# A four-layer cross-attention and mixture-of-experts kernel: middle attentions re-ordered, layernorms and a close by halves, rows numbered by partition, offsets in one load

## The chip, the cores and the metric

The kernel runs on one core of a Trainium2 chip. The metric is the device time of one launch in microseconds (us): lower is better. TensorE (PE, with its weight loads shown as PEld), VectorE (DVE), ScalarE (ACT), GpSimd (POOL) and SyncE (SP) run their own instruction streams and meet at semaphores. Each instruction waits in its stream for the one before it.

## The reference

A residual stream x of 4 batches x 256 tokens x 128 features goes through four layers. Each is a cross attention over a context of 64 rows per batch and a feed-forward network with experts, each behind a layernorm:

```python
x = x + _L0_xattn_ref(_layernorm(x), ctx, ctx, bias, ...)      # 16 heads of 8, additive bias, softmax
x = x + _L0_ffn_ref(_layernorm(x), Wr, W1, W2)                 # 8 experts, top 2, capacity 320, relu
x = x + _L1_xattn_ref(ctx, ctx, _layernorm(x), fm_w, fm_b, fc_w, fc_b)
    # per head z = fm_w @ h + fm_b, features [exp(z), exp(-z)] of q, k and v; softmax(q k / sqrt(128)) v
x = x + _L1_ffn_ref(_layernorm(x), gate_w, Wg, Wu, Wd, Sg, Su, Sd)
    # each of 16 experts takes its 128 best tokens; gelu(g) * u; plus a shared expert
x = x + _L2_xattn_ref(_layernorm(x), ctx, ctx, mask, ...)      # scores clipped to +-50, exp / sum
x = x + _L2_ffn_ref(_layernorm(x), Wr, Wg, Wu, Wd, Sg, Su, Sd) # 16 experts, top 2, dense; plus a shared one
x = x + _L3_xattn_ref(_layernorm(x), ctx, ctx, ...)            # 16 heads of 64
x = x + _L3_ffn_ref(_layernorm(x), router_w, gate_w, up_w, down_w)  # 8 experts, argmax, silu(g) * u
```

with `_layernorm(x) = (x - mean) / sqrt(var + 1e-5)`.

## The kernel before

x stays on chip as 8 tiles of 128 tokens (T = 8; a batch is two tiles, a half is four). The order of each engine's instructions is written out by hand, one function per stage and engine, with semaphores between them. So what stands ahead of an instruction in its engine's stream matters as much as what it needs. Stages by the timeline, in us: attention 0 to 65, routing and FFN 0 to 169, reload of its results to 178, attention 1 to 260, route 1 to 314, FFN 1 to 384, reload and keys for layer 3 to 401, attention 2 to 448.5, FFN 2 to 519, its close to 525, attention 3 to 580, route 3 to 596, offsets to 607, FFN 3's blocks to 657.

*Layernorm.* DVE takes the statistics of each tile (L1630, L1634, or L1625, L1626), writes var + eps (`ve`, L1639), POOL raises it to -0.5 for all 8 tiles at once (`rsqrt`, L446), and DVE normalises tile by tile.

*Fillers.* `keep_busy(n, bank)` (L959) issues n matmuls of zeros, 128 x 512 in bf16, into an unused bank. They compute nothing.

*Attention 1.* By batch b. PE turns x (L761), projects to features (L767); ACT takes exp of them (L1428). `row_scores` (L779) makes scores by row in two halves k through the same two banks; after each DVE takes maxima (L1817), and the second half waits for the first one's. The maxima are turned (L787), scores are made again by column with the maxima subtracted (L797, L802), ACT takes exp (L1439), and `values` (L817) makes the weighted values in bank 6 and then the sums of exps in bank 7. DVE takes the reciprocal of the sums (L1823) and the product (L1827), PE projects (L826, L827), DVE adds to x (L1833) and takes the statistics of the batch's two tiles. PE's order around batch b is query(b+2), scores(b+1), project(b), features(b+2), row_scores(b+2), values(b+1), turn_max(b+2). At its start it waits for the second half of FFN 0's results (`y_in1`) and runs 11 fillers.

*Attention 2.* The same way without features and maxima: query (L858, L863), scores (L872), ACT's exp (L1471), DVE's clip on the exps (L1863), values and sums (L885, both in bank 6), reciprocal (L1868), product (L1872), project (L894, bank 7), residual (L1878). Ahead of it PE computes the keys of layer 3 (L642, L653), DVE copies the one (L1702) and ACT the other (L1301); then 14 fillers.

*Routing.* L925 makes logits, DVE shifts them by their maximum (L1928), ACT takes exp (L1481), DVE normalises and, in layers 0 and 2, picks the two best by chains of small operations (L1906 to L1942). In layer 1 each expert looks for its 128 best tokens in ten rounds: DVE compares with candidates (L2069), PE counts (L941), DVE picks (L2076). The shared expert's matmuls (L1172, L1179) stand before and beside the rounds, and DVE adds its output to x in the last two.

*FFN 0, 1 and 3* write normalised rows to DRAM, gather them by index with POOL's indirect transfers (L469, L491, L543), and scatter results back the same way. A token's row number in DRAM is t x 128 + p (tile t, partition p). FFN 3 has 15 blocks of 128 slots; the weights of each block are picked by an offset that PE's sequencer reads from `eoff` into a register (L1117), once `block_experts` is signalled; then 8 fillers, and the blocks' first transpose (L1126).

*FFN 2* is dense, by 18 steps of up (L1075) and down (L1079). Then both sums are closed, ACT copies them (L1301), PE turns them (L970), and DVE adds each half to x (L2201) and takes its statistics. The signal `banks_free` after that starts PE's 5 fillers of attention 3, whose first transpose is L679.

## Time and profile before

| | us |
|---|---|
| median of three timed runs | 677.31 |
| lowest, highest | 671.31, 681.23 |
| the profiled execution, its own time | 664.8 |
| its span, first to last instruction | 663.1 |
| PE busy | 496.4 (75%) |
| PE weight loads (beside PE) | 306.3 (46%) |
| DVE busy | 309.8 (47%) |
| ACT busy | 180.1 (27%) |
| POOL busy | 148.8 (22%) |

The page divides the span in 40 slices of 16.6 us and gives the busy share of each in tenths:

```profile
PE   5997974898378876865688886857999578743884
DVE  4895765034415544576122232556344379650221
ACT  2552451342122210200233343312121144301431
POOL 5000001775200000000466521000000023305542
PEclk9997597799658775787999998768999899955998
```

Slice 11 is where FFN 0's results are reloaded, slices 12 to 16 are attention 1, 25 to 27 attention 2, 37 the offsets of FFN 3. PEclk is the TensorE clock that was granted, in tenths of full speed: 5 is the low level throughout, 9 or more the high one. A busy PE at the low level spends twice the time on the same work.

### The profile page before, as it was taken

The page shows a single profiled execution, that of the slowest core. Times are in us where ns is not written, and L with a number is a line of the kernel's source. Part 1 is how long each engine was busy: PE and PEld are TensorE (multiplying, and loading weights), DVE is VectorE, ACT ScalarE, POOL GpSimd, SP SyncE. Part 2 cuts the span into 40 slices and gives each one's busy share as a digit, 9 for nine tenths or more (in the row PEclk, how much of TensorE's full clock was granted, in tenths as well). Part 3 has the DMA queues.
Part 4 walks back from the last instruction along what each step waited for, and adds up shares of the span by engine and source line. Part 5 has one row for each costly group of instructions (what it writes and reads, how often), then busy time and mean ns, then how long its engine had stood idle before and what let it go on. Part 6 is the DMA issues. An engine that isn't in the chain of part 4 may idle for free.

```text
span 663.1 us, 7544 instructions
## 1 busy us (share of the span) xinstructions
PE 496.4 (75%) x2654; PEld 306.3 (46%) x2664; DVE 309.8 (47%) x784; ACT 180.1 (27%) x367; POOL 148.8 (22%) x167
## 2 busy tenths in 40 slices
PE   5997974898378876865688886857999578743884
PEld 2676652575144543443355543424333246631663
DVE  4895765034415544576122232556344379650221
ACT  2552451342122210200233343312121144301431
POOL 5000001775200000000466521000000023305542
PEclk9997597799658775787999998768999899955998
DMA  7600200344200000102377530002010400022110
GB/s 239 215 1 6 61 1 9 87 149 168 70 1 0 1 1 0 37 1 79 113 228 229 129 96 0 1 1 101 13 36 24 168 1 0 1 64 72 47 31 4
DMA packets 30103, 41.22 MB, mean 62 GB/s; under 512 B 7220, under 2 KB 23997, under 8 KB 29938
## 3 DMA queue, kind: packets, MB, share of 16 engines
q1 hardware_dynamic: 24482, 33.17, 15.2%
q0 software_dynamic: 5296, 7.17, 5.2%
q8 instruction: 22, 0.36, 0.2%
q10 hardware_dynamic: 288, 0.39, 0.2%
q14 instruction: 15, 0.12, 0.1%
HBM read 33.80 MB, written 7.63 MB: 62 GB/s over the span
## 4 chain that ended last, share of the span: by engine, by line
PE 43%; DVE 26%; issue 14%; DMA 5%; ACT 5%; POOL 5%; POOLq 0%; SPq 0%; DVEq 0%; ACTq 0%
PE bank L1029 3%; DMA xgr<-rows,idx 3%; PE bank L1037 3%; PE bank L779 3%; PE bank L1075 2%; DVE ind L2069 2%; PE bank L1079 2%; PE bank L885 2%; DVE PT L1823 2%; POOL rstd L446 2%; PE bank L1071 2%; PE bank L817 2%; PE bank L941 2%; PE bank L872 2%; DVE lg L1745 2%
## 5 line engine op out<-in xcount | busy, mean ns | idle before, releaser
L446 POOL TENSOR_TENSOR rstd<-ve,neghalf 128x8 f32<-128x8 f32 x8 | 13.2, 1654 | 283.6 <-DVE ve L1639 283.6
L959 PE MATMUL bank<-zero_bf 128*128 128x512 bf16 x95 | 32.6, 502 | 33.3 <-issue 12.7
L1301 ACT ACTIVATE PT<-bank 128x512 f32<-128x512 f32 (+1 forms) x52 | 28.4, 579 | 32.0 <-PE bank L1241 20.6
L2156 DVE SCALAR_TENSOR_TENSOR PT<-bank,xgr,sg 128x512 f32<-128x512 f32 x16 | 12.0, 751 | 48.6 <-ACT sg L1536 48.6
L959 PEld LDWEIGHTS bank<-zero_bf 128*128 128x128 bf16 x104 | 11.6, 121 | 48.4 <-issue 23.3
L684 PE MATMUL bank<-A,xaT 128*128 128x512 f32 x64 | 32.2, 628 | 2.4 <-ACT xaT L1301 2.4
L2185 DVE TENSOR_TENSOR PT<-bank,sg 128x352 f32<-128x352 f32 x15 | 7.9, 524 | 45.5 <-ACT sg L1570 45.5
L491 POOL DMA_INDIRECT xgr<-rows,idx x16 | 15.7, 982 | 56.3 <-DVE idx L1999 51.7
L469 POOL DMA_INDIRECT A<-rows,from_row x15 | 14.4, 962 | 49.4 <-DVE from_row L1985 45.1
L1029 PE MATMUL bank<-pr,wbig 128*128 128x320 f32 x64 | 24.7, 473 | 0.7 <-ACT pr L1301 0.7
L2112 DVE TENSOR_TENSOR PT<-bank,sg 128x512 f32<-128x512 f32 x16 | 11.1, 692 | 29.7 <-ACT sg L1487 29.7
L1391 ACT ACTIVATE pr<-lg 128x1024 f32<-128x1024 f32 x16 | 16.9, 1057 | 26.8 <-DVE lg L1745 26.8
L1817 DVE TENSOR_REDUCE mx<-bank 128x8 f32<-128x512 f32 x16 | 10.3, 686 | 28.8 <-PE bank L779 28.8
L1487 ACT ACTIVATE sg<-bank 128x512 f32<-128x512 f32 x18 | 10.6, 597 | 46.8 <-PE bank L1075 46.8
L1037 PE MATMUL bank<-PT,wbig 128*128 128x320 f32 x64 | 22.8, 444 | 0.0
L525 POOL TENSOR_TENSOR pr<-pr,rden 128x1024 f32<-128x1024 f32 x8 | 15.2, 1901 | 32.8 <-DVE rden L1758 32.8
L941 PE MATMUL bank<-ind,ones_bf 128*128 128x56 bf16 (+1 forms) x160 | 11.2, 221 | 14.6 <-DVE ind L2069 14.6
L475 POOL DMA_INDIRECT choices<-eo,to_row x20 | 19.7, 984 | 10.3 <-DVE eo L2120 5.5
L779 PE MATMUL bank<-A,kblk 64*128 64x256 f32 x64 | 17.1, 605 | 6.5 <-DVE mx L1817 3.4
L698 PE MATMUL bank<-ident,pr 128*128 128x128 f32 x128 | 17.2, 277 | 4.4 <-ACT pr L1391 2.7
L1301 ACT ACTIVATE xaT<-bank 128x128 f32<-128x128 f32 x31 | 8.4, 273 | 43.8 <-PE bank L1126 24.6
L1512 ACT ACTIVATE PT<-bank 128x320 f32<-128x320 f32 x32 | 14.0, 437 | 22.5 <-PE bank L1029 22.5
(395 smaller groups left out, 1155.6 us busy)
## 6 DMA issues: line engine op xcount, KB each, us to landing
wbig<-in_fw SPq DMA_DIRECT2D x16, 768.0 KB, 4.5
wbig<-in_fw SPq DMA_DIRECT2D x8, 544.0 KB, 5.3
wbig<-in_fw SPq DMA_DIRECT2D x8, 512.0 KB, 3.7
wbig<-in_aw SPq DMA_DIRECT2D x1, 2048.0 KB, 9.4
rows<-xn SPq DMA_DIRECT2D x3, 512.0 KB, 3.7
...
```

Of the source, the lines that this page charges most:

```text
L446: pool.tensor_tensor(out=rstd[:, :], in0=ve[:, :], in1=neghalf[:, :], op=ALU.pow).then_inc(S("ln_rstd"), 1)
L475: pool.indirect_dma_start(yd, bass.IndirectOffsetOnAxis(to_row[:, 5 * p + k:5 * p + k + 1], 0), eo0[:, 5 * (p % 2) + k, :], None, bounds_c ...
L491: pool.indirect_dma_start(xgr[:, e % 4, :], None, rowd, bass.IndirectOffsetOnAxis(idx[:, e:e + 1], 0)).then_inc(S(f"gathered{e % 4}"), 16)
L684: mm = pe.matmul(bank[2 * j + c][:, :], xaT[:, j, :], A[:, b, 8 * c:8 * c + 8, :].rearrange("p h k -> p (h k)"), start=True, stop=True)
L698: mm = pe.transpose(bank[4 + half][:, q * P:(q + 1) * P], pr[:, j, 2 * c:2 * c + 2, :].rearrange("p h k -> p (h k)"), ident[:, :])
L779: mm = pe.matmul(bank[4 + g][:, c * 256:(c + 1) * 256], qf1[half, b % 2, c, k * P:(k + 1) * P], kb1[half, c, b, :, :].rearrange("p j k -> ...
L941: mm = pe.matmul(bank[4][:, 0:7 * e], ones_bf[:, :], ind[:, t, 0:7 * e], start=(t == 0), stop=(t == T - 1))
L959: pe.matmul(bank[free][:, :], zero_bf[:, 0:P], zero_bf[:, :], start=True, stop=True)
L1029: pe.matmul(bank[s % 2][:, 0:CAP[0]], wring[:, e % 4, m * P:(m + 1) * P], xgT0[:, (e // 2) % 2, cols], start=True, stop=True).then_inc(S(" ...
L1037: pe.matmul(bank[6 + e % 2][:, 0:CAP[0]], wring[:, e % 4, 512 + m * P:512 + (m + 1) * P], hh[:, s % 4, 0:CAP[0]], start=(m == 0), stop=(m ...
L1301: return act.activation(dst, src, ACT.Copy)
L1391: act.activation(pr[:, j], lg[:, j], ACT.Exp, scale=(1.0 if layer == 0 else SCALE[layer])).then_inc(S("at_p"), 1)
```

## The change

- DRAM rows of all layers are numbered p x 8 + t, so that a partition's rows lie side by side; the index arithmetic changes with it (one step becomes three in layer 0, one matmul more in layer 1), and FFN 0's results are loaded by two transfers instead of four.
- The layernorms before attentions 1, 2 and 3 take statistics, var + eps and pow by halves; the second half's statistics stand after the first tiles are normalised.
- Attention 1: sums become a group of their own ahead of the second half of row_scores, values follow, features(b+2) goes ahead of project(b), batch statistics go behind the next batch's maxima. Sixteen fillers instead of 11, from `y_in0` on, and 16 more between the first groups.
- Attention 2: sums (now bank 7) before values, turning apart from queries, exps ahead of the next queries on ACT, the exp table loaded ahead by a dummy activation (`table_try`), 8 fillers instead of 14, from the first half's arrival on, and half-size fillers between groups. DVE's copies of layer 3's keys go to ACT, ACT's copies of the values of attention 2 to DVE.
- Routing: in layers 0 and 2 the two best are found on the shifted logits, ahead of the wait for exp; layer 3 loses a copy. Fillers (8 instead of 5) stand ahead of the wait for the attention's end. In layer 1 four of the shared expert's eight first matmuls move beside the rounds, its adds to x from rounds 8 and 9 to the start of FFN 1.
- FFN 2 is closed by halves, the first before the last down.
- FFN 3: eight more fillers after the ranks, the fifteen register loads become one call, and PE waits for `pos` too. Tables for Gelu, Silu and Exp are loaded ahead by dummy activations in layers 1 to 3.

The core of the diff:

```diff
-                    sp.dma_start(ysum[:, c, 4 * h:4 * h + 4, :],
-                                 yd[c * TOK + h * HALF:c * TOK + (h + 1) * HALF, :].rearrange("(t p) d -> p t d", p=P)
-                                 ).then_inc(S(f"y_in{h}"), 16)
...
+                sp.dma_start(ysum[:, :, 4 * h:4 * h + 4, :], yd.rearrange("(p c t) d -> p c t d", c=2, t=T)[:, :, 4 * h:4 * h + 4, :]
+                             ).then_inc(S(f"y_in{h}"), 16)
...
+            rowd_t = rowd.rearrange("(p t) c -> p t c", p=P)
+            xd_t = xd.rearrange("(p t) d -> p t d", p=P)
...
-                pool.wait_ge(S("ln_var"), n + 1)
-                pool.tensor_tensor(out=rstd[:, :], in0=ve[:, :], in1=neghalf[:, :], op=ALU.pow).then_inc(S("ln_rstd"), 1)
-                pool.wait_ge(S("ln_rstd"), n + 1)
+                for h in range(2 if n in BY_HALVES else 1):
+                    tiles = slice(4 * h, 4 * h + 4) if n in BY_HALVES else slice(0, T)
+                    pool.wait_ge(S("ln_var"), ln_count(n, h))
+                    pool.tensor_tensor(out=rstd[:, tiles], in0=ve[:, tiles], in1=neghalf[:, tiles], op=ALU.pow).then_inc(S("ln_rstd"), 1)
+                    pool.wait_ge(S("ln_rstd"), ln_count(n, h))
...
+                pe.wait_ge(S("eo"), 36)
...
-                pe.wait_ge(S("y_in1"), 32)
-                keep_busy(11, 7)
+                pe.wait_ge(S("y_in0"), 16)
+                keep_busy(16, 7)
...
-                def row_scores(b):
+                def row_scores(b, k):
...
-                    for k in range(2):
...
-                                    mm.then_inc(S("s1_mm"), 1)
+                    for c in range(2):
+                        for g in range(2):
+                            if k and c == 0:
...
+                def sums(b):
+                    if b >= 1:
+                        pe.wait_ge(S("res2"), 2 * b)
+                    for c in range(2):
...
+                            mm = pe.matmul(bank[7][32 * i:32 * i + 32, c * 256:(c + 1) * 256], ones1[:, :, :].rearrange("p s n -> p (s n)"),
+                                           pe2[b % 2][:, i, c * 256:(c + 1) * 256], start=True, stop=True, skip_group_check=True)
+                    mm.then_inc(S("o2_mm"), 1)
...
                     if b >= 1:
                         pe.wait_ge(S("ob2"), b)
-                        pe.wait_ge(S("res2"), 2 * b)
-                    for dst, den in ((bank[6], False), (bank[7], True)):
-                        for c in range(2):
...
                 query(0)
+                keep_busy(2, 6)
                 features(0)
-                row_scores(0)
+                keep_busy(4, 6)
+                row_scores(0, 0)
+                keep_busy(3, 6)
+                row_scores(0, 1)
+                keep_busy(5, 6)
                 turn_max(0)
+                keep_busy(2, 6)
                 for b in range(-1, B):
                     if b + 2 < B:
                         query(b + 2)
                     if b + 1 < B:
                         scores(b + 1)
+                    if b + 2 < B:
+                        features(b + 2)
                     if b >= 0:
                         project(b)
                     if b + 2 < B:
-                        features(b + 2)
-                        row_scores(b + 2)
+                        row_scores(b + 2, 0)
+                    if b + 1 < B:
+                        sums(b + 1)
+                    if b + 2 < B:
+                        row_scores(b + 2, 1)
                     if b + 1 < B:
                         values(b + 1)
...
                 pe.wait_ge(S("projT"), 16 + 4)
                 pe.wait_ge(S("a_sb"), 22 + 8)
-                pe.wait_ge(S("x_back"), 48)
-                keep_busy(14, 7)
-                query(0)
+                pe.wait_ge(S("x_in"), 48)
+                keep_busy(8, 6)
+                turn(0)
+                keep_half(4)
+                queries(0)
+                keep_half(4)
+                turn(1)
                 scores(0)
-                query(1)
+                queries(1)
                 pe.wait_ge(S("v2"), 4)
+                keep_half(10)
                 for b in range(B):
                     if b + 1 < B:
                         scores(b + 1)
+                    if b + 2 < B:
+                        turn(b + 2)
+                    if b == 0:
+                        keep_half(6)
+                    sums(b)
                     values(b)
                     if b + 2 < B:
...
+                    pe.matmul(bank[6][:, 0:256], zero_bf[:, 0:P], zero_bf[:, 0:256], start=True, stop=True)
+
             def open_sums():
 
                 for c in range(2):
...
                     if q > 2:
                         down(q - 1, wring[:, ((q - 3) // 2) % 2, 2 * P:3 * P])
+                close_sum(0)
+                turn_sums(0)
                 down(17, wring[:, 1, 2 * P:3 * P])
+                close_sum(1)
+                turn_sums(1)
+
+            def close_sum(c):
+                pe.matmul(bank[6 + c][:, :], zero_bf[:, 0:P], zero_bf[:, :], start=False, stop=True, skip_group_check=True
+                          ).then_inc(S("f_sum"), 1)
+
+            def turn_sums(c):
+                pe.wait_ge(S("f_yT"), c + 1)
+                for t in range(4 * c, 4 * c + 4):
+                    mm = pe.transpose(bank[c][:, (t % 4) * P:(t % 4 + 1) * P],
+                                      yT[:, c, (t % 4) * P:(t % 4 + 1) * P], ident[:, :])
+                mm.then_inc(S("f_out"), 1)
...
+                keep_busy(8, 6)
 
...
+                _, base = nc.values_load_multi_w_load_instructions(eoff[0:1, 0:BLOCKS], engines=(mybir.EngineType.PE,),
+                                                                   min_val=0, max_val=7 * F3_UNIT)
                 pe.wait_ge(S("w3_in"), 16 * 8)
+                pe.wait_ge(S("pos"), 1)
...
+                up(0, 1)
 
             def shared1_beside(i):
                 up, down = shared1()
-                if i < 4:
-                    up(2 + i // 2, i % 2)
...
+                    pe.wait_ge(S("const"), 2)
+                    keep_busy(8, 3)
                     pe.wait_ge(S("banks_free_a"), layer + 1)
-                    pe.wait_ge(S("const"), 2)
-                    keep_busy(5, 3)
...
-                        act.wait_ge(S("o2_mm"), 4 + b - 1)
+                        act.wait_ge(S("o2_mm"), 8 + 2 * b - 2)
                     for i in range(4):
                         act.wait_ge(S("s2_mm"), 16 + 4 * b + i + 1)
                         act.activation(pe2[b % 2][:, i, :], bank[i][:, :], ACT.Exp, scale=SCALE[2]).then_inc(S("exp2"), 1)
+
+                act.activation(table_try[:, :], neghalf[:, 0:1], ACT.Exp)
+                turned(0)
+                queries(0)
+                turned(1)
+                exps(0)
+                queries(1)
+                for b in range(B):
                     if b + 2 < B:
-                        query(b + 2)
+                        turned(b + 2)
+                    if b + 1 < B:
+                        exps(b + 1)
+                    if b + 2 < B:
+                        queries(b + 2)
...
+                act.activation(table_try[:, :], neghalf[:, 0:1], ACT.Gelu)
+
...
+                    if layer == 3 and t in (0, 4):
+                        dve.wait_ge(S("ln_rstd"), ln_count(6, t // 4))
...
+                batch_stats(B - 1)
 
             def attention2():
                 lo, hi = math.exp(-CLIP), math.exp(CLIP)
 
...
+                    if b in (0, 2):
+                        dve.wait_ge(S("ln_rstd"), ln_count(4, b // 2))
                     for k in range(2):
...
-                    dve.wait_ge(S("o2_mm"), 4 + b + 1)
-                    dve.reciprocal(rd2[:, b % 2, :], bank[6][:, 256:512]).then_inc(S("rd2"), 1)
+                    dve.wait_ge(S("o2_mm"), 8 + 2 * b + 1)
+                    dve.reciprocal(rd2[:, b % 2, :], bank[7][:, 0:256]).then_inc(S("rd2"), 1)
                     dve.wait_ge(S("rd2"), 4 + b + 1)
+                    dve.wait_ge(S("o2_mm"), 8 + 2 * b + 2)
                     if b >= 2:
                         dve.wait_ge(S("y2_mm"), 4 + b - 1)
...
+                first_of_marked(layer, dst)
+
+            def first_of_marked(layer, dst):
+
+                e = E[layer]
                 chain(dve.tensor_reduce(rm[:, :], ev(rk, layer), AX.X, ALU.max))
                 chain(dve.tensor_tensor(dst, ev(rk, layer), rm[:, :].unsqueeze(2).broadcast_to([P, T, e]), ALU.is_equal))
 
@@ -1919,13 +2010,21 @@
                 dve.wait_ge(S("router"), layer + 1)
                 z = bank[5 if layer < 3 else 2][:, 0:n].rearrange("p (t e) -> p t e", t=T)
                 if layer == 3:
-                    chain(dve.tensor_copy(ev(rp, 3), z))
```

## Rows read from the trace of the kernel before

**Rows 1.** Cores' view
```profile
core 0: 663.1 us, clock 0.844
```

**Rows 2.** Windows: length, busy us (instructions) of PE, PEld, DVE, ACT, POOL; PEclk, DMA
```profile
174.00:180.00 6.00, 4.47 (x10) 1.49 (x11) 3.94 (x19) 0.00 (x0) 1.67 (x1) 0.50 0.00 0
204.00:210.00 6.00, 4.54 (x54) 3.24 (x46) 4.29 (x3) 1.85 (x4) 0.00 (x0) 1.00 0.00 0
210.00:217.00 7.00, 5.35 (x20) 3.24 (x20) 2.73 (x8) 1.66 (x3) 0.00 (x0) 0.56 0.00 0
```

**Rows 3.** Timeline, layer 2's routing: start, length, engine, line, what; idle before
```profile
456.04 0.29 DVE L1930 TENSOR_REDUCE rr<-rl 128x8 f32<-128x128 f32 x1 [0.38 <-ACT rl L1481]
...
460.81 0.29 DVE L1942 TENSOR_TENSOR rq<-r,rp 128x128 f32<-128x128 f32 x1
```

**Rows 4.** Timeline, start of attention 1
```profile
171.97 1.42 DVE L2148 TENSOR_TENSOR x<-lg,x 128x512 f32<-128x512 f32 x2 [5.99 <-DMA lg<-choices]
...
180.04 0.66 PE L761 MATMUL bank<-ident,PT 128*128 128x128 f32 x2 [1.01 <-DVE PT L1808]
...
184.02 2.08 PE L779 MATMUL bank<-A,kblk 64*128 64x256 f32 x8 [0.78 <-ACT kblk L1428]
```

**Rows 5.** Timeline, middle of attention 1
```profile
198.72 1.13 PE L779 MATMUL bank<-A,kblk 64*128 64x256 f32 x8 [0.78 <-ACT kblk L1428]
...
204.33 3.36 DVE L1823 RECIPROCAL PT<-bank 128x512 f32<-128x512 f32 x1
...
221.89 3.36 DVE L1823 RECIPROCAL PT<-bank 128x512 f32<-128x512 f32 x1 [1.22 <-PE bank L817]
...
250.62 3.36 DVE L1823 RECIPROCAL PT<-bank 128x512 f32<-128x512 f32 x1 [2.78 <-PE bank L817]
```

**Rows 6.** Timeline, route 1, first search round
```profile
268.26 5.67 PE L1172 MATMUL bank<-xnT,sh_sb 128*128 128x512 f32 x8
...
270.91 1.09 DVE L2069 TENSOR_TENSOR ind<-rq,cand 128x896 bf16<-128x896 f32 x1
...
273.77 0.56 PE L941 MATMUL bank<-ind,ones_bf 128*128 128x112 bf16 x8
```

**Rows 7.** Timeline, close of FFN 2 and start of attention 3
```profile
521.02 0.69 DVE L2201 TENSOR_TENSOR x<-bank,x 128x512 f32<-128x512 f32 x1 [3.48 <-PE bank L970]
...
525.19 2.32 PE L959 MATMUL bank<-zero_bf 128*128 128x512 bf16 x5 [3.77 <-DVEq L2235]
...
527.70 0.44 PE L679 MATMUL bank<-ident,xa 128*128 128x128 f32 x1 [0.20 <-DVE xa L1723]
```

**Rows 8.** Timeline, attention 2
```profile
395.97 1.08 ACT L1301 ACTIVATE A<-bank 128x512 f32<-128x512 f32 x2 [0.76 <-PE bank L653]
...
401.51 0.58 PE L858 MATMUL bank<-ident,wbig 128*128 128x128 f32 x2 [1.18 <-DVE wbig L1857]
...
406.87 1.28 ACT L1471 ACT_TABLE_LOAD   x1
...
415.92 1.76 DVE L1868 RECIPROCAL PT<-bank 128x256 f32<-128x256 f32 x1 [4.46 <-PE bank L885]
...
428.44 3.28 PE L872 MATMUL bank<-PT,wbig 32*128 32x256 f32 x16
...
443.40 1.76 DVE L1868 RECIPROCAL PT<-bank 128x256 f32<-128x256 f32 x1 [3.02 <-PE bank L885]
```

**Rows 9.** One line's instructions: L1117; duration ns min/median/max, first and last start
```profile
L1117 PEldq TENSOR_LOAD <-eoff x15: 295/302/492, 596.2 to 605.7; - x15
L1117 PEldq FUSED_REGOPS  x15: 146/146/165, 596.8 to 606.1; - x15
L1117 PEldq SEQ_ASSERT  x15: 18/18/24, 597.0 to 606.3; - x15
```

**Rows 10.** Timeline, start of FFN 3's blocks
```profile
606.74 3.19 PE L959 MATMUL bank<-zero_bf 128*128 128x512 bf16 x7 [10.95 <-issue]
...
609.73 0.42 PE L1126 MATMUL bank<-ident,Vb 128*128 128x128 f32 x1
```

**Rows 11.** DMA issues: what, engine, operation, count, us from issue to landing
```profile
xgr<-rows,idx POOLq DMA_INDIRECT x16, 3.1
```

301 lines of the change are left out of this document (163 added, 138 removed).

## The prediction

> **What bounds the kernel now.** I read the cores' view first: one core, a span of 663.1 us and a mean granted TensorE clock of 0.844 [rows 1]. The profiled execution took 664.8 us by its own time, 1.7 us around its span. The three timed runs have a median of 677.31 us, 12.5 us above the profiled one. My sum is made against 664.8, and 12.5 is added to it at the end. I then read the page's tenths: the two middle attentions and the routings show low PE digits and low clock digits, while the FFNs are dense, and the chain that ended last goes from PE to DVE to ACT and back. No engine bounds the span; chains of small steps between PE, ACT and DVE do, and PE's steps cost double where its clock is at the low one of its two levels (1.2 and 2.4 GHz). The windows show both in one stage: ten fillers in 4.47 us at a granted 0.50, 54 matmuls in 4.54 us at 1.00, then 20 in 5.35 us at 0.56 [rows 2]. So I went by timeline through each edited stretch.
>
> **The change part by part.**
>
> *Routing, layers 0 and 2.* The second choice is taken from the shifted logits, so its operations run while the exp is on its way. In layer 2, 16 chained DVE operations stand from the sum of the exps (after 0.38 idle) to the last one [rows 3], 0.32 apart. I count 14 after: 0.65 and the 0.38 of the wait, 1.0. Layer 0 has smaller operations (0.8 by the same count) and pays two more small ones for from_row, 0.3. Sum **1.5** (0.5 to 2.3).
>
> *Attention 1, start.* Before, eleven fillers run from about 174.1 (ten of them in the 4.47 us above) and the first transposes are at 180.04 [rows 4]. Now sixteen fillers start when the first half of ysum has landed, where DVE's first add on it stands at 171.97 [rows 4]. At 0.447 each (4.47/10) sixteen take 7.2 us: the transposes can go at about 178.6 even if the clock stays low. The half pow and norm_x(0), behind two adds and one half's statistics, are done by then (estimate: 176.6). Gain **1.5** (0.5 to 3.4, the last if the clock rises while the fillers run).
>
> *Attention 1, prologue.* All of it was at the low level: L779 took 2.08 us against 1.13 at the high level [rows 4, 5]. The prologue's groups (L761, L767, L779, L787, L797, L802) would save about 5 us together when warm. Sixteen more fillers stand in it, 3.4 us warm or 7 cold, and PE idles about 3.9 us there now between groups. So warm they are hidden, gain 5; cold they stick out by 3. I take **3.5**, mostly warm.
>
> *Attention 1, the two middle periods.* The reciprocals start at 204.33 and 221.89, 17.5 us apart [rows 5]. That period is a ring: reciprocal 3.4, product 0.7, projection 2.1, features 1.9, ACT 0.7, scores 2.1, maxima 0.8, scores 2.7, values with sums 3.1. The change takes features out of it (they go before project, under the reciprocal) and the second half of values (the reciprocal needs sums alone), and puts batch_stats, 1.05 us of DVE, in: it now stands between the maxima and the reciprocal. Worked through: 6.3 to the end of project, scores 1.1 (2.1 cold), sums 1.05 (1.75), second scores 1.7 (2.7), last maximum 0.8, statistics 1.05, norm_x 0.6: 12.6 warm, 16 cold. I take 15.0 for each, because the clock has fallen in this ring before [rows 2]: 2 x 2.5 = **5.0** (-2 to 9).
>
> *Attention 1, tail.* The last reciprocal (250.62 [rows 5]) no longer waits for values(3), 1.9, and part of the projection is warm: **2.4** (1 to 3.5).
>
> *Route 1.* The first round's L941 starts at 273.77, behind eight L1172 matmuls of 5.67 us from 268.26 [rows 6]. DVE's ind for it was ready at 272.0 (270.91 + 1.09). Four remain of the eight, so PE is free at 271.1: 1.75. The other four go beside the rounds, where PE waits for DVE; two adds of x (0.69 each [rows 7]) leave the rounds for the start of experts1. With half of them, **2.5** (1 to 5). With them a store of x and a weight load on SP's queue fall among the first gathers of FFN1: **-0.5**.
>
> *Attention 2.* Its start hangs on ACT's last keys copy (395.97 + 1.08) and then fourteen fillers and pow; the transposes are at 401.51 [rows 8]. With the first half's pow early and eight fillers, 397.1 + 2.0 = 399.1: 2.4. Then ACT copied queries(1) ahead of the exps, and loaded a table at 406.87 for 1.28, before the first exp; the reciprocal came at 415.92. With the table loaded ahead and the exps first they start at about 402.5, 4.4 earlier beyond the start's gain (5.7 in all by 408.16); turn(2) and six half fillers now stand before sums(0), 1.1, and sums saves the second half, 1.9. The first reciprocal is then at 407.7 to 410; I take 409.0, 6.9. From it to the last (443.40) are 27.5 us in three periods. A period of after is reciprocal 1.8, product 0.4, project 0.8, scores 3.3 [rows 8] (about 2 warm), turn 0.7, sums 1.9 (0.9): 8.9 cold, 6.2 warm; before it was 9.6 cold. Three take 22.0 (16.7 to 26): 5.5. Sum **12** (5 to 16). The keys copies on ACT instead of DVE cost nothing: PE is full there, and ACT has room beside its 1.08 per pair. If ACT's order delays one, 0.5.
>
> *FFN 2 closed by halves.* Now DVE adds half 0 from 521.02 and releases PE's five fillers at 525.19, only after both halves' statistics; L679 is at 527.70 [rows 7]. After, half 0 is turned before the last down, and the release stands behind the second add, at about 521.1. The five fillers (2.32) then set the end rather than pow: 523.6. Gain **4.1** (3.5 to 5.9).
>
> *FFN 3, the offsets.* PE's sequencer spends 596.2 to 606.3 on fifteen triples: a load of 302 ns, register operations of 146, an assert of 18, 0.68 apart [rows 9]. Eight fillers follow (seven in 3.19), and block 0's transpose is at 609.73 [rows 10]. One load instruction takes the place of fifteen, but the bounds are still given, so I let the fifteen checks stand: 15 x (0.146 + 0.018) = 2.5 us at least, 15 x 0.38 = 5.7 if each keeps its slot without the load. Middle 4.1, and 0.4 for the load: 4.5 for 10.1, gain **5.6**. The ends are 9.5 (no checks, 0.3 to 0.6 for the load) and 0.5 (the load is taken apart again). By the Trainium skill ("Runtime: NRT & Kernel Launch", Instruction fetch mechanics) a register load costs about 200 ns per register even in bulk; by that page the fifteen would still cost 3.0 us, and this gain would be an estimated 3.0. The trace has 302 ns for a load by itself and nothing for a bulk one.
>
> *Route 3* loses a copy: **0.3**. *The row numbering* turns 512-byte pieces of the direct transfers into 2 and 4 KB runs; none of them ends a wait I counted, but the first ysum half: 0 (0 to 0.5). Table loads moved off the path in the FFNs: 0, since ACT idles there.
>
> Sum: 1.5 + 1.5 + 3.5 + 5.0 + 2.4 + 2.5 - 0.5 + 12 + 4.1 + 5.6 + 0.3 = 37.9. 664.8 - 37.9 = 626.9 for the profiled execution, and with 12.5 a median of 639.4, so **639**.
>
> **Rivals.**
>
> A, *the clock doesn't rise or hold.* Ten fillers at a stretch ran at a granted 0.50 [rows 2]. Then the prologue costs 3 instead of gaining 3.5 (-6.5), the middle periods save 1.5 each (-2.0), the tail 1.4 (-1.0), attention 2 saves 7 (-5), route 1 1.5 (-1): 15.5 less, **655**. For it: 16 fillers cold were hardly more than 10. Against it: the clock rose by itself in attention 1 before 204 [rows 2], with less work on PE. The Trainium skill ("TensorE: Matmul & The Clock Gate", What's actually happening) has the low level as the default, which activity releases; the trace agrees that it isn't load that lowers it.
>
> B, *the offsets gain nothing.* The multi load is issued as fifteen loads with their checks: 5.1 less, **644**. All triples are alike now and the bounds are kept; against it only that the edit asks for one instruction.
>
> C, *the other side: the gathers and scatters get slower.* With rows numbered by partition, tokens of one tile lie 4 KB apart rather than next to each other, and some 100 indirect transfers use the new numbers. In FFN 1 each of 16 experts waits for its gather, 3.1 us to land [rows 11]. To eat 38 us each would have to land 2.4 us later, 5.5 for 3.1. Then **677 or more**. Against it: the indirect transfers fetch one row per descriptor either way.
>
> D, *the upside.* Clock high through both attentions (4 + 4 + 1.5) and no checks (3.9): 13 more, **626**.
>
> **How the numbers follow.** Forecast 0.55, A 0.20, B 0.10, D 0.10, C 0.02, and 0.03 for another new wait. The forecast's own range is 630 to 648. The range wanted reaches over B, most of A and D: 622 to 658. A measurement of this kernel tells some 2% from no change, that is 663.8 us; all but C and the new waits lie below, a bad A with B (660) close to it: faster 0.93, same 0.05, slower 0.02.
>
> **What would show each step.** The timeline: transposes L761 near 178.6 (times before minus 1.5 for what precedes), reciprocals L1823 some 15 apart and L1868 some 7.3 apart; a granted clock over 0.8 in the windows of both; L941's first start 2 us after L925's group and not behind L1172; L679 about 4 us sooner after the last L1079, with fillers ending just before it; under the load's line one TENSOR_LOAD and fifteen asserts within 4.5 us. Wrong would be: a clock of 0.50 with more fillers in it (A), fifteen loads (B), gathers landing at over 4 us (C), or batch_stats on DVE as the releaser of a reciprocal that PE's sums had long been ready for.

## The result, and the profile after

The changed kernel takes 633.91 us, the median of four runs (633.52 to 634.16). The kernel before, measured beside it, takes 674.31 (667.29 to 681.23). The ratio is 0.947, with a 95% interval of 0.942 to 0.952: 40 us, or 5.3%, faster. The forecast was 639, within 622 to 658.

Below are the cores' view and two rows of the page, busy tenths and granted clock, of the changed kernel.

```profile
core 0: 632.0 us, clock 0.891
```

```profile
PE   4898874659869877866588788869999879765884
...
PEclk9998699589969996777799999976999989976998
```

The span fell by 31.1 us from the 663.1 of [rows 1], where my sum had 37.9, while the median fell by 40.4. The table cuts both traces at the same instructions and sets each stage's change beside its term in the forecast. A copy of y is DVE's copy of one expert's result in FFN 0; there are eight. The forecast column adds up to 38.3 and not 37.9, since attention 2's parts (2.4, 4.5 and 5.5) make 12.4, where the sum took 12.

| stretch, from where to where (us) | before | after | gained | forecast |
|---|---|---|---|---|
| start to first gather of FFN 0 | 112.1 | 112.9 | -0.8 | 0.5 |
| FFN 0, to the last copy of y | 48.8 | 58.3 | -9.5 | 0 |
| reload, to attention 1's first transposes | 19.2 | 17.4 | 1.8 | 1.5 |
| prologue, to the first reciprocal | 24.3 | 18.4 | 5.9 | 3.5 |
| the two middle periods | 35.1 | 25.0 | 10.1 | 5.0 |
| tail, to route 1's transposes | 23.4 | 21.0 | 2.4 | 2.4 |
| route 1, to the first gather of FFN 1 | 51.3 | 50.0 | 1.3 | 2.5 |
| FFN 1 and reload, to attention 2's first transposes | 87.4 | 91.9 | -4.5 | 1.9 |
| attention 2, to its first reciprocal | 14.4 | 8.9 | 5.5 | 4.5 |
| its three periods | 27.5 | 19.4 | 8.1 | 5.5 |
| its end and FFN 2, to DVE's last product | 73.4 | 74.6 | -1.2 | 1.0 |
| close, to attention 3's first transpose | 10.9 | 5.4 | 5.5 | 4.1 |
| attention 3 and route 3, to the offsets | 68.3 | 65.2 | 3.1 | 0.3 |
| offsets, to the first block | 13.7 | 9.8 | 3.9 | 5.6 |
| blocks, to the end | 53.4 | 53.9 | -0.5 | 0 |

The table compares one execution with one. The fourteen profiles show how far a stage moves without an edit to it. The second profile of the kernel before has 27.6 for the two middle periods, 47.7 for route 1 and 61.0 for FFN 0, and agrees with the first within 0.2 in attention 2, in the end of it up to attention 3, in attention 3 and in the offsets. FFN 1 takes 87.2 to 92.0 in the ten profiles of changed kernels in which its start is not edited, 87.4 and 87.3 before.

Both attentions gave more than forecast, and 9.5 us went in FFN 0, where next to nothing was changed. That place first. The timeline of the changed kernel around it (start, length, engine, line, what, and in brackets the idle time before with its releaser), and the same two copies of y in the profile of before:

```profile
129.13 0.49 DVE L2230 COPY yT<-bank 128x320 f32<-128x320 f32 x1 [17.18 <-PE bank L1061]
...
131.06 0.70 PE L1061 MATMUL bank<-PT,wbig 128*128 128x320 f32 x2
...
133.32 0.49 ACT L1334 ACTIVATE pr<-bank 128x384 f32<-128x384 f32 x1 [4.55 <-issue]
...
138.92 0.44 ACT L1565 ACTIVATE PT<-bank 128x320 f32<-128x320 f32 x1 [3.11 <-remote]
...
139.50 1.41 PE L1053 MATMUL bank<-pr,wbig 128*128 128x320 f32 x2 [7.74 <-issue]
...
141.05 0.61 DVE L2221 TENSOR_SCALAR eo<-bank,A 128x128 f32<-128x128 f32 x2 [11.42 <-remote]
...
143.65 0.49 DVE L2230 COPY yT<-bank 128x320 f32<-128x320 f32 x1 [1.99 <-PE bank L1061]
```

```profile
128.27 0.49 DVE L2129 COPY yT<-bank 128x320 f32<-128x320 f32 x1 [17.14 <-PE bank L1037]
...
133.35 0.49 DVE L2129 COPY yT<-bank 128x320 f32<-128x320 f32 x1 [2.62 <-PE bank L1037]
```

PE runs dry at 131.76. ACT moves in steps of 2 to 4 us and DVE waits 11.4, most of it for signals whose sender the profile does not name (`remote`), though PE had issued the transposes and matmuls that they need. POOL alone goes on issuing gathers. From the first copy of y to the second are 14.5 us here, 5.1 in the profile of before. I call it the hole. The view of the DMA queues for 118 to 146 us names what moved data meanwhile:

```profile
q0 software_dynamic: 584, 1.25, 25.1%
q1 hardware_dynamic: 230, 0.88, 9.6%
```

No instruction queue is among them, in this profile or in any other that has the hole. So a wait for instructions to be loaded, at least one that the DMA records would show, is not its cause.

Attention 1's ring in the changed kernel, timeline: three of the four reciprocals, and what stands ahead of the second.

```profile
206.95 3.35 DVE L1897 RECIPROCAL PT<-bank 128x512 f32<-128x512 f32 x1
...
213.30 0.49 DVE L1908 TENSOR_TENSOR x<-bank,x 128x128 f32<-128x128 f32 x2 [2.27 <-PE bank L846]
...
214.26 1.07 PE L827 MATMUL bank<-pr,ones 128*32 128x256 f32 x16
214.40 1.29 DVE L1891 TENSOR_REDUCE mx<-bank 128x8 f32<-128x512 f32 x2 [0.61 <-PE bank L792]
...
216.91 1.29 DVE L1891 TENSOR_REDUCE mx<-bank 128x8 f32<-128x512 f32 x2 [1.22 <-PE bank L792]
218.12 0.28 DVE L1682 BATCH_NORM_STATS2 st<-x 128x6 f32<-128x128 f32 x1
...
219.71 3.35 DVE L1897 RECIPROCAL PT<-bank 128x512 f32<-128x512 f32 x1
...
231.96 3.36 DVE L1897 RECIPROCAL PT<-bank 128x512 f32<-128x512 f32 x1
```

The periods are 12.8 and 12.3 us, against 17.6 and 17.5 [rows 5]. The sums (L827) are done at 215.3 and the reciprocal starts at 219.71, with no idle time noted: it waits for DVE's own maxima, statistics and normalisation, which stand ahead of it in DVE's stream. The prediction named this as a sign of being wrong, though its own 12.6 us for a warm period already counted that chain. The windows of the two periods (length; busy us and instructions of PE, PEld, DVE, ACT, POOL; granted clock; DMA share; GB/s) answer to [rows 2]:

```profile
207.00:220.00 13.00, 11.00 (x103) 7.02 (x102) 8.72 (x16) 3.90 (x8) 0.00 (x0) 1.00 0.01 1
220.00:232.00 12.00, 10.48 (x103) 6.62 (x102) 7.72 (x13) 3.51 (x7) 0.00 (x0) 1.00 0.01 1
```

The clock is at its high level throughout. FFN 1's start in the changed kernel, and then in the kernel before, from the first gather to the first scatter of a result:

```profile
302.93 1.04 POOL L504 DMA_INDIRECT xgr<-rows,idx  x1 [50.50 <-DVE idx L2095]
303.32 0.34 SPq L353 DMA_DIRECT2D residual<-x  x1
303.71 0.43 SPq L317 DMA_DIRECT2D wbig<-in_fw  x1
...
307.59 0.47 PE L1264 MATMUL bank<-ident,xgr 128*128 128x128 f32 x1 [3.96 <-DMA xgr<-rows,idx]
...
320.14 1.62 POOL L511 DMA_INDIRECT residual<-eo,idx  x1 [12.40 <-DVE eo L2267]
```

```profile
314.09 1.04 POOL L491 DMA_INDIRECT xgr<-rows,idx  x1 [51.69 <-DVE idx L1999]
...
316.68 0.33 PE L1223 MATMUL bank<-ident,xgr 128*128 128x128 f32 x1 [1.90 <-DMA xgr<-rows,idx]
...
325.68 1.62 POOL L498 DMA_INDIRECT residual<-eo,idx  x1 [6.79 <-DVE eo L2163]
```

The first block is turned 4.7 us after its gather's issue, 2.6 before, and from gather to scatter are 17.2 us, 11.6 before. FFN 2's close, to be held against [rows 7]:

```profile
502.01 1.25 PE L1007 MATMUL bank<-zero_bf 128*128 128x512 bf16 x5 [0.84 <-DVEq L2344]
502.11 0.60 DVE L1788 TENSOR_SCALAR xa<-x,mv,rstd 128x128 f32<-128x128 f32 x2 [0.22 <-POOL rstd L459]
...
503.10 0.27 PE L693 MATMUL bank<-ident,xa 128*128 128x128 f32 x1
```

And the offsets, the instructions of the line that replaced L1117 [rows 9]:

```profile
L1157 PEldq FUSED_REGOPS  x15: 146/146/165, 570.3 to 574.3; - x15
L1157 PEldq SEQ_ASSERT  x15: 18/18/28, 570.6 to 574.5; - x15
L1157 PEldq TENSOR_LOAD <-eoff x1: 1767/1767/1767, 568.5 to 568.5; - x1
```

One load of 1.77 us, but the fifteen checks stayed, 0.29 apart, 4.2 us.

### The profile page after: what moved, and what is told of

It reads as the page before. It is cut to its first block, busy times and chain, and to the rows that moved or that the text cites. A ratio compares the mean times of both kernels' runs of the same rounds, so it can differ in the third digit from the quotient of the medians.

```text
span 632.0 us, 7686 instructions
## 1 busy us (share of the span) xinstructions
PE 492.5 (78%) x2724; PEld 299.8 (47%) x2724; DVE 307.0 (49%) x782; ACT 182.9 (29%) x375; POOL 151.3 (24%) x173
## 3 DMA queue, kind: packets, MB, share of 16 engines
q1 hardware_dynamic: 20482, 33.17, 15.6%
## 4 chain that ended last, share of the span: by engine, by line
PE 41%; DVE 24%; issue 20%; DMA 6%; ACT 4%; POOL 4%; POOLq 0%; SPq 0%; DVEq 0%; ACTq 0%
DMA xgr<-rows,idx 3%; PE bank L1053 3%; PE bank L1099 3%; PE bank L1061 3%; PE bank L1095 3%; PE bank L1103 3%; DVE ind L2170 2%; DVE PT L1897 2%; PE bank L1007 2%; PE bank L989 2%; PE bank L792 2%; DVE mx L1807 2%; DVE rden L1821 2%; DVE lg L1810 2%; POOL rstd L459 1%
## 5 line engine op out<-in xcount | busy, mean ns | idle before, releaser
L459 POOL TENSOR_TENSOR rstd<-ve,neghalf 128x4 f32<-128x4 f32 (+1 forms) x11 | 15.0, 1368 | 243.3 <-DVE ve L1696 149.5
L1007 PE MATMUL bank<-zero_bf 128*128 128x512 bf16 x139 | 45.4, 483 | 14.3 <-issue 8.0
L698 PE MATMUL bank<-A,xaT 128*128 128x512 f32 x64 | 32.1, 626 | 2.7 <-ACT xaT L1334 2.7
L1007 PEld LDWEIGHTS bank<-zero_bf 128*128 128x128 bf16 x139 | 15.6, 119 | 36.7 <-issue 22.8
L2290 DVE TENSOR_TENSOR PT<-bank,sg 128x352 f32<-128x352 f32 x15 | 7.9, 525 | 40.4 <-issue 20.3
L482 POOL DMA_INDIRECT A<-rows,from_row x15 | 14.5, 965 | 49.6 <-DVE from_row L2081 45.3
L1061 PE MATMUL bank<-PT,wbig 128*128 128x320 f32 x64 | 23.4, 453 | 0.0
L1334 ACT ACTIVATE pr<-bank 128x384 f32<-128x384 f32 (+1 forms) x23 | 10.7, 472 | 37.9 <-issue 23.2
L712 PE MATMUL bank<-ident,pr 128*128 128x128 f32 x128 | 17.6, 281 | 4.3 <-ACT pr L1432 2.7
L567 POOL DMA_INDIRECT result<-lg,to_row x15 | 15.0, 1002 | 22.7 <-DVE lg L2295 17.4
L989 PEld LDWEIGHTS bank<-ind,ones_bf 128*128 128x128 bf16 x160 | 8.4, 108 | 25.1 <-DVE ind L2170 24.8
## 6 DMA issues: line engine op xcount, KB each, us to landing
choices<-rowpad SPq DMA_DIRECT2D x1, 1024.0 KB, 14.6
```

The costliest lines, as they stand in the source:

```text
L459: pool.tensor_tensor(out=rstd[:, tiles], in0=ve[:, tiles], in1=neghalf[:, tiles], op=ALU.pow).then_inc(S("ln_rstd"), 1)
L698: mm = pe.matmul(bank[2 * j + c][:, :], xaT[:, j, :], A[:, b, 8 * c:8 * c + 8, :].rearrange("p h k -> p (h k)"), start=True, stop=True)
L712: mm = pe.transpose(bank[4 + half][:, q * P:(q + 1) * P], pr[:, j, 2 * c:2 * c + 2, :].rearrange("p h k -> p (h k)"), ident[:, :])
L989: mm = pe.matmul(bank[4][:, 0:7 * e], ones_bf[:, :], ind[:, t, 0:7 * e], start=(t == 0), stop=(t == T - 1))
L1007: pe.matmul(bank[free][:, :], zero_bf[:, 0:P], zero_bf[:, :], start=True, stop=True)
L1061: pe.matmul(bank[6 + e % 2][:, 0:CAP[0]], wring[:, e % 4, 512 + m * P:512 + (m + 1) * P], hh[:, s % 4, 0:CAP[0]], start=(m == 0), stop=(m ...
```

## The experiments

They ran in three sets, each on another chip. Within a set the kernels share the chip and the runs of the kernel before, whose medians were 673.94 us (670.4 to 677.2), 659.59 (650.7 to 666.6) and 668.71 (663.3 to 683.8). The changed kernel itself was run in the third set alone. So in the first set the measure is its 633.91 from the runs ahead, where the kernel before had 674.31, and in the second a kernel that comes close to it.

**The kernel before once more** (first set, no edit).

> The kernel before, unchanged, profiled a second time. Its timed runs lie from 667.3 to 681.2 us, its profiled execution at 664.8, while the changed kernel's four runs lie within 0.7 us and its profile shows a hole of some 9 us in FFN 0 (PE from 131.76 to 139.50, DVE from 129.62 to 141.05) that the profile of before does not have. Theory (holes come in most executions, in both kernels): this profile has a span some 5 to 15 us over 663.1, and the difference stands in one or two places where PE, ACT and DVE all pause though nothing they need is missing. Rival (the hole belongs to the changed kernel alone): span within 2 us of 663.1 and the last eighth of FFN 0 at the same distance from its first gather, 48.8 us.

Measured: 664.8 us, span 663.1, to the digit the first profile's. But it is another 664.8. Its timeline has the hole:

```profile
138.86 0.44 ACT L1512 ACTIVATE PT<-bank 128x320 f32<-128x320 f32 x1 [3.14 <-remote]
...
139.62 0.61 DVE L2120 TENSOR_SCALAR eo<-bank,A 128x128 f32<-128x128 f32 x2 [10.16 <-remote]
```

From the first copy of y to the second are 15.1 us, 10 more than in the first profile. In return attention 1's reciprocals are 13.8 us apart, not 17.5, which makes 7.4 us in the two middle periods, and route 1 is 3.6 shorter. The windows of the two periods, to be held against a granted 0.70 to 0.72 in the first profile:

```profile
214.00:228.00 14.00, 10.89 (x110) 6.85 (x100) 8.76 (x16) 3.51 (x7) 0.00 (x0) 1.00 0.01 1
228.00:242.00 14.00, 10.89 (x108) 6.85 (x100) 8.30 (x13) 3.51 (x7) 0.00 (x0) 1.00 0.01 1
```

So the hole is no part of the change: the expectation's first half holds, its span does not. And the old ring has two speeds by the clock. FFN 0 takes 9.5 to 12.7 us more with the hole than without it in the nine profiles that have it. By these numbers I estimate 674 to 678 us for an execution of the kernel before with the hole and a slow ring, and 652 to 655 for one with neither.

**The store of x behind the first gathers** (first set).

```diff
-            sp.wait_ge(S("x_shared"), 2)
-            sp.dma_start(xd_t, x[:, :, :]).then_inc(S("x_stored"), 16)
             load_weights(1, 3, 3)
+            sp.wait_ge(S("x_shared"), 2)
+            sp.wait_ge(S("gathered1"), 48)
+            sp.dma_start(xd_t, x[:, :, :]).then_inc(S("x_stored"), 16)
```

The edit also puts the weight load of expert 3, which had stood right behind the store, ahead of the gathers.

> The changed kernel with one edit on SP's queue: the weights of expert 3 are loaded before x is waited for, and the store of x is issued only when the gathers of experts 0 and 1 have landed. Theory (the store of 512 KB and the weight load at 303.3 and 303.7 us hold up the first gather, PE idles 4 us, its clock falls and two experts run cold; from the first gather to the first scatter went 17.2 us after and 11.6 before): 17.2 becomes about 11.6, the kernel 5 to 6 us faster than the changed one, 628.3. Rival (the first experts are slow because fewer fillers or the added matmul left the clock low, or the new row numbers slow the gathers): the first gather's landing stays at 4.6 us or the clock low, and the time stays within 1.5 us of 633.9.

Measured: 630.5 us (629.0 to 634.9), 3.4 less than the changed kernel's 633.91; one of the four runs is above that. The timeline of FFN 1's start:

```profile
302.56 1.04 POOL L505 DMA_INDIRECT xgr<-rows,idx  x1 [48.86 <-DVE idx L2096]
...
305.21 0.33 PE L1265 MATMUL bank<-ident,xgr 128*128 128x128 f32 x1 [1.96 <-DMA xgr<-rows,idx]
```

The first block is turned after 2.65 us again, as before, so the two transfers and not the new row numbers held the gather up; which of the two, the run can't say. From first gather to first scatter are 13.1 us, not 17.2, and not 11.6: half of the first expert's matmuls are still at the low clock. The mechanism holds. Its size is less sure. In the ten profiles of changed kernels with both transfers in place the block is turned 4.2 to 5.1 us after the gather's issue, and from gather to scatter are 14.6 to 17.6 us. Against 13.1 here and 13.0 in the kernel with three edits below, that is 1.5 to 4.6.

**No fillers inside the two attentions** (first set): the calls `keep_busy(2, 6)`, `(4, 6)`, `(3, 6)`, `(5, 6)`, `(2, 6)` of attention 1's prologue and all of `keep_half` are left out.

> The changed kernel without the fillers inside the prologue of attention 1 (2, 4, 3, 5, 2) and without the half-size fillers of attention 2 (4, 4, 10, 6); the sixteen and eight at the stages' starts stay. Theory (the fillers hold the clock high, and that is a large part of what both attentions gained): the prologue is 2 to 4 us longer and the two middle periods of attention 1 go from 12.5 to 14 or 16 us, attention 2's periods from 6.4 to 8; 8 to 15 us slower in all, 642 to 649. Rival (the order alone does it: PE has less idle time in the new ring, so the clock rises and holds without them): within 2 us of 633.9, or up to 2 us faster since the fillers' own 6.2 us are gone.

Measured: 637.9 us (635.4 to 638.9), 4.0 more than the changed kernel. The windows of the two middle periods of attention 1, reciprocals at 212.35, 225.11 and 237.35:

```profile
212.00:225.00 13.00, 11.07 (x102) 6.91 (x102) 8.72 (x16) 3.90 (x8) 0.00 (x0) 1.00 0.01 1
225.00:237.00 12.00, 10.72 (x100) 6.82 (x100) 7.79 (x12) 3.24 (x7) 0.00 (x0) 1.00 0.01 1
```

The periods are what they were, 12.8 and 12.2, and attention 2's are 6.5 on average, as with fillers. The rings hold the clock by their order. What the fillers buy lies in the prologue: 20.0 us from the first transposes to the first reciprocal, not 18.4. The theory falls; the rival is nearer, though 4 us is more than it allowed. The profile, the fastest of its four runs, is 1.7 longer than the changed kernel's; the rest of the 4.0 is unplaced.

**The fifteen loads apart again** (first set).

```diff
-                _, base = nc.values_load_multi_w_load_instructions(eoff[0:1, 0:BLOCKS], engines=(mybir.EngineType.PE,),
-                                                                   min_val=0, max_val=7 * F3_UNIT)
+                base = [pe.value_load(eoff[0:1, h:h + 1], min_val=0, max_val=7 * F3_UNIT) for h in range(BLOCKS)]
```

> The changed kernel with fifteen single register loads in place of the one call, as before. Theory (the call saves what the profile says: 6.0 us from eoff to the last assert instead of 10.1): 4.1 us slower, 638.0, all of it between eoff and the first block. Rival (it is hidden, since block 0's gather must land anyway at 572.8 and PE's clock is cold after): under 2 us.

Measured: 641.5 us (640.4 to 641.8). In its trace the first block is turned 13.6 us after the offsets, 9.8 in the changed kernel: 3.8, as expected. The whole is 7.6 slower; of the rest, 1.8 stand ahead of the offsets, where the two kernels are the same, and 0.9 in the blocks. Stages move by that much between executions without an edit.

**The gathers of FFN 0 in groups** (second set).

```diff
-                for p in range(4):
+                for p in range(2):
                     for k in range(5):
                         gather(p, k)
                 for p in range(4):
+                    if p < 2:
+                        pool.wait_ge(S("x_Tc"), 2 * p + 4)
+                        for k in range(5):
+                            gather(p + 2, k)
                     for k in range(5):
                         scatter(p, k)
```

> The changed kernel, in which POOL issues the ten gathers of the last four experts of FFN 0 in two groups of five, each only once PE has turned the blocks of the pair before, with the scatters of finished blocks between, instead of all twenty gathers in a row. Five of six profiles so far (one of two of the kernel before, all four of changed ones) have the hole at 130 to 141 us, while POOL issues its last eight gathers, and it ends 1 to 4 us after the last. Theory (a train of gathers beside the first weight load holds up the signals between PE, ACT and DVE): no hole, first copy of y to the second 5.1 us as in the one profile without it and not 14, the kernel some 9 us faster than the changed one, 625. Rival 1 (the hole comes from something else at that time, instruction loading or the weight load alone): it stays, and the time is 634 or, since gathers now come later, up to 3 us more. Rival 2 (the hole goes, but the later gathers make PE wait as long): 630 to 636 without a common pause of PE, ACT and DVE.

Measured: 629.5 us, 7.7 more than the next kernel, whose FFN 0 is timed as the changed one's. It has no hole, but neither has any other kernel of this set, so it says nothing on the hole's cause. It shows what late gathers cost: the sixth copy of y comes 11.2 us after the fifth, where 4.6 to 5.1 is the rule.

**The first weight load of FFN 0 later** (second set).

```diff
-                sp.wait_ge(S("x_down"), 4 * (u - 4) + 4)
+                sp.wait_ge(S("x_down"), 8 if u == 4 else 4 * (u - 4) + 4)
```

> The changed kernel, in which SP issues the first weight load of FFN 0 (expert 4) one expert later, together with that of expert 5. The hole begins within 1 us of the moment at which that load was issued, in every profile that has it. Theory (gathers alone do it): the hole stays where it is, 634 +- 1.5. Rival (the weight load among the gathers does it): the hole moves to the later load or goes, 625 to 628 if it goes.

Measured: 621.8 us (620.4 to 624.7), no hole, copies of y 5.1 apart. The two kernels below left FFN 0 alone and have no hole here either. In this set nothing had it, so this too is open. It does show that a train of gathers with the weight load among them is not enough to bring the hole on: those two kernels have both. The kernel can serve as the set's measure of the changed one, since the load it moves ends no wait.

**Features behind the projection again** (second set): in attention 1's loop, `features(b + 2)` stands after `project(b)`.

> The changed kernel with features(b+2) of attention 1 behind project(b) again, as before; all else as changed. Theory (at the high clock the new order is worth what it takes out of the ring, and features is most of that; the second profile of the kernel before, whose clock stayed high there, has the old order's periods at 13.8 us and the new order has 12.2 to 12.8): the two middle periods become 13.4 to 13.9 and the kernel 2 to 3 us slower, 636.5. Rival (the order matters by the clock: with PE idle again under the reciprocal the clock falls): periods of 16 to 17.5, the kernel 8 us or more slower.

Measured: 627.1 us (623.0 to 630.5), 5.3 more. The reciprocals stand at 196.95, 211.63 and 228.14: 14.7 and 16.5. The windows:

```profile
197.00:212.00 15.00, 11.15 (x103) 7.03 (x102) 8.81 (x16) 3.90 (x8) 0.00 (x0) 1.00 0.00 1
212.00:228.00 16.00, 12.72 (x99) 7.49 (x98) 7.49 (x12) 3.46 (x7) 0.00 (x0) 0.79 0.00 1
```

In the first period, at the high clock, it costs 1.9: the features' own time. In the second the clock falls and it costs 4.3. Theory and rival are both right, one period each. With features ahead of project the clock is at its high level through both periods in all eleven profiles. With features behind it, it is so in one of three (the kernel before once more), and falls in the other two. So the high clock goes with the new order in every profile, but the old order can have it too.

**Batch statistics behind the residual again** (second set): `batch_stats(b)` stands after `residual(b)`, and not after the next maxima.

> The changed kernel with the batch statistics of attention 1 right behind the residual again, as before, instead of behind the next maxima. In the trace of the changed kernel DVE stands idle 0.6 us between residual and maxima, and the statistics, 1.05 us, stand between the last maximum and the reciprocal. Theory (DVE's chain sets the ring now): each of the three periods gets 0.6 us shorter, 12.2 to 11.7, the kernel 1.8 us faster, 632. Rival (the maxima come later by 0.5, the second scores with them, and PE becomes the end of the ring): no difference, within 0.5 us per period either way.

Measured: 619.8 us (617.1 to 621.6), 2.0 less than the set's measure, 621.8 (620.4 to 624.7), and the runs overlap. Periods of 12.2, 11.7 and 8.1 instead of 12.8, 12.2 and 9.0: 0.6, 0.6 and 0.9, as the theory had it. So within the ring this detail of the change was a loss. Of its 2.1 us the two profiled executions keep 0.3: from the last reciprocal of attention 2 to attention 3's first transpose go 81.1 us here and 79.4 in the other.

**The changed kernel once more** (third set, no edit).

> The changed kernel, unchanged, once more, as the measure for the three runs beside it on the same chip. Theory (the hole in FFN 0 depends on the chip: on the chip of the first runs five of six profiles had it, on the chip of the second set none of four, with kernels whose FFN 0 is the same): either 633.5 with the hole, or about 622 without it, and the kernel before shifts with it by the same 9 to 14 us. Rival (it depends on small differences of the kernels): hole or not is not the same for the four kernels of this set.

Measured: 633.7 us (632.0 to 635.8), the hole in its profile and in those of the three kernels beside it. The hole goes with the set of runs, not with the kernel: it is in nine of ten profiles of the first measurement and of sets one and three, in both kernels, and in none of four in set two, whose kernel before is 9 to 14 us faster. Whether it is the chip or something else that differs between the sets is not shown; the tenth profile, without it, is the first of the kernel before.

**Without the bounds checks** (third set): `skip_runtime_bounds_check_because` is given to the one load.

> The changed kernel without the fifteen bounds checks behind the one register load of FFN 3 (no other part of the computation is left out; the offsets are bounded by the operation that makes them). Theory (PE's sequencer spends 0.29 us on each check, 4.2 in all, on the path): the first block 4.2 us earlier, unless its gather, which landed about 3 us after its issue at 1.3 us behind eoff, then holds it up; 4 us faster than the changed kernel. Rival (the single load of 1.77 us and the gather hide most of it): under 2 us.

Measured: 633.0 us (631.3 to 635.6), 0.7 less, which these runs can't tell from nothing. The timeline shows the step gained:

```profile
570.86 3.48 PE L1007 MATMUL bank<-zero_bf 128*128 128x512 bf16 x8 [2.37 <-DVE to_row L2138]
...
574.13 0.41 PE L1169 MATMUL bank<-ident,Vb 128*128 128x128 f32 x1
```

The first block comes 5.4 us after the offsets, not 9.8. But from it to the last scatter are 49.6 us, not 47.2 or 48.0 as in the two profiles of the changed kernel. Two waits of 3.1 us in the blocks, again on an unnamed sender, make it up:

```profile
583.11 0.49 ACT L1335 ACTIVATE pr<-bank 128x384 f32<-128x384 f32 x1 [3.08 <-remote]
...
601.93 0.49 ACT L1335 ACTIVATE pr<-bank 128x384 f32<-128x384 f32 x1 [3.06 <-remote]
```

ACT's wait at this place is else 1.03. In the twelve profiles with the checks the stretch is 46.6 to 48.1 us; six of them, the second of the kernel before among them, have one or two waits for an unnamed sender there, of at most 1.5 us. In the other kernel without the checks, the next below, it is 49.5, with a wait of 3.07. Two of two speak for the earlier start, or the missing checks, bringing the waits on; how is open.

**Three edits together** (third set): the store behind the gathers, no checks, statistics behind the residual.

> The changed kernel with three edits together: the store of x behind the first two gathers of FFN 1, no bounds checks, and attention 1's batch statistics right behind the residual. Theory (three separate places of the path: 4.5, 4 and 2 us): 10 us faster than the changed kernel on the same chip. Rival (gains are given back: a shorter wait leaves the clock lower in the stage after it): 6 us or less.

Measured: 628.7 us (624.3 to 633.7), 5.0 less than the changed kernel beside it; 0.942 (0.937 to 0.947) of the kernel before, where the changed one is at 0.948 (0.943 to 0.953). In the profiles the gap is 10.8 (623.2 against 634.0), but these are the second fastest of six runs and the slowest of four. Each edit shows in its place: 13.0 us from gather to scatter, periods of 12.2 and 11.7, 5.5 us from the offsets to the first block. The median gives half of it, so the theory's 10 us is not borne out and the rival's 6 or less is. It is the fastest of this set, but with runs that spread over 9 us, and the two intervals overlap.

**Sums directly ahead of the values** (third set): in attention 1's loop, `sums(b + 1)` stands after the second half of `row_scores`.

> The changed kernel with the sums of attention 1 directly ahead of the values again, behind the second half of row_scores; all else as changed. My forecast of the middle periods counted the sums' place as a gain of up to 1.9 us per period. Theory after the trace (the reciprocal waits for DVE's own chain of maxima, statistics and normalisation, which ends 3.4 us after the sums): no difference, periods within 0.3 us of 12.2 to 12.8, within 1 us in all. Rival (as forecast): 1 to 2 us per period, 3 to 6 us slower.

Measured: 633.1 us (631.4 to 638.2), 0.6 less than the changed kernel. Periods 12.8, 12.2 and 9.0: the same. The place of the sums is worth nothing in attention 1 as long as DVE's chain ends after them.

## Why the prediction was right, and where not

That 639 lies near 633.9 is in part luck. The sum was made from [rows 1]: 664.8 less 37.9 is 626.9. The profiled execution took 633.8, 6.9 more. The hole's 9.4, which I knew nothing of, is in it, and without the hole the time would lie 2.5 below my sum. That is roughly what remains of stages that gave 15.6 us more than forecast and others that gave 13.3 less: the terms' errors cancelled. The 12.5 that I added at the end, from the profile to the median, I took over without a reason, and it happened to cover the hole. A likely reason, argued and not shown since only profiles show a hole, is that the profile that I read lacks the hole and most timed executions on that chip have it. Of the 5.5 between 639.4 and 633.9, 3.0 is the median of before, 677.31 of three runs and 674.31 of four; 2.5 is the gain, 40.4 and not 37.9.

- **Attention 1, middle periods** (5.0, measured 10.1). The ring was worked out step by step as 12.6 us warm, and it is 12.8 and 12.3. The mis-sized step is the choice of 15.0, "because the clock has fallen in this ring before": in eleven profiles of the new order it did not fall. The cold end was mis-added too: its steps make 15.3 and not 16. Features ahead of project fills time in which PE had idled under the reciprocal; with features put back the clock fell in the second period, though the old order held it once. Against that second profile of the kernel before the two periods gain 2.6 and not 10.1, so what this term is worth hangs on which way an execution of the old ring takes. One assignment was wrong: I took the second half of values, 1.9, as part of what a period saves. The run with the sums last shows nothing of it, since DVE's chain ahead of the reciprocal ends 4 us after the sums.
- **Prologue** (3.5, measured 5.9). It ran warm, as the upper bound of 5 supposed. Without the inner fillers 1.6 of the 5.9 is lost. The rest I put down to the sixteen at the start, which no run took out. I had written that 16 cold ones are hardly more than 10. They run from 182.91 to 188.72, 5.8 us and not 7.2: the first eleven start some 0.43 us apart, the last five 0.22, and the granted clock is 0.50 from 183 to 187 and 1.00 from 188 to 190.
- **Rival A** is answered: the clock rose and held. It rested on ten fillers at 0.50 [rows 2]. The Trainium skill ("TensorE: Matmul & The Clock Gate", What's actually happening) has it that activity releases the low level; the traces agree in that it rose under the sixteen fillers and that with features put back, and PE idle for longer in the same ring, it fell from 1.00 to 0.79.
- **Attention 2** (10.0 of the 12, measured 13.6). Its first reciprocal came 8.9 after the start and its periods are 5.9, 6.3 and 7.2, where I had 6.2 warm and 8.9 cold and chose between. (Three of these make 18.6 to 26.7, not the 16.7 to 26 that I wrote.) The granted clock over the three periods is 0.91, against 0.63 before. The same mis-sizing as above. What the fillers add here is measured, nothing in the periods; no run takes the rest of the new order apart, so it is argued from the timeline.
- **FFN 1** (1.9, measured -4.5). The failed step is the -0.5 for the moved store and weight load. I named the collision and gave it no row. The gather landed 2.1 later, PE went idle and the granted clock from 308 to 318 is 0.55: 17.2 us to the first scatter instead of 11.6. With the two transfers moved 13.1 are left. The whole stage's -4.5 is at the bad end of what ten profiles show, -4.6 to +0.2; so by itself the table's number is no measure of the step.
- **Route 1** (2.5, measured 1.3). The first search round starts 10.9 us after the stage's first transposes in the profile that I read and 8.2 in the changed kernel, but 7.7 in the second profile of the kernel before: there the router's matmuls and the eight L1172 ran at the high clock, and the round did not wait for them. The stage takes 51.3 and 47.7 before, 46.6 to 50.7 in the twelve profiles of changed kernels. That the change gained anything here is not shown.
- **The close** (4.1, measured 5.5). The five fillers are the last thing ahead of the transpose, as forecast, at 503.10. They take 1.25, not 2.32, since PE, idle for 0.84 us ahead of them and not 3.77, comes warm out of FFN 2. That warmth goes on: attention 3's first L698 group takes 1.99, where L684 took 3.52. That is 1.5 of the 3.1 that attention 3 and route 3 gained, where I had 0.3; the rest I have not placed.
- **The offsets** (5.6, measured 3.9). The checks stayed, as I supposed, at 4.2 us (I had 4.1). The single load takes 1.77, where I put 0.4 from one load's 302 ns [rows 9]. That is 118 ns per register. The rule of the Trainium skill ("Runtime: NRT & Kernel Launch", Instruction fetch mechanics), some 200 ns for each even in bulk, would make an estimated 3.0; the trace is between, and a little nearer to the page than to me. Rival B, fifteen loads, did not come.
- **Routing** (1.0 in layer 2, measured -1.2 with the rest of its stage). The chain from the shift to the first cast is 4.78 us, 5.76 before: the 1.0, exactly. It was given back beside it. The eight fillers now run before the attention's end is waited for, PE's weight loads then idle 2.0 ahead of its transposes, 1.0 before, and the router's matmuls take 3.38 instead of 1.99. They take 2.8 to 3.5 in all twelve profiles of changed kernels. I had costed the fillers' move at nothing. That the move is the cause is argued; no run puts them back. Layer 0 (0.5, measured -0.8) is not explained. Two rows of after and one of before:

```profile
431.14 0.84 PEld L966 LDWEIGHTS bank<-ident,xn 128*128 128x128 f32 x4 [2.00 <-issue]
...
433.04 3.38 PE L973 MATMUL bank<-wr_sb,xnT 128*128 128x16 f32 x16
```

```profile
453.02 1.99 PE L925 MATMUL bank<-wr_sb,xnT 128*128 128x16 f32 x16
```

- **Rival C**, slower indirect transfers, is out at its first step: in FFN 0 the first block is turned 5.7 us after its gather's issue in both kernels, in FFN 1 2.65 after with the two transfers moved and 2.6 before. Its sign, a gather landing at over 4 us, did show in FFN 1 (4.6), but from another cause. The train of scatters of FFN 1, 58.0 us before, is 57.3 to 60.8 in the changed ones; a small loss can't be excluded.
- **Left open**: what causes the hole. Shown is that it belongs to both kernels, to some sets of runs, to one place, and that ACT, DVE and then PE wait in it, most of it for signals without a named sender. That gathers beside a weight load bring it on was only argued, and they are not enough. The two runs meant to tell fell in a set without it.
